# Keys and low halves of the second sorted edge list, made at the end of the first graph layer's loop instead of at the head of its dense part

## The reference

```python
# 1: first graph layer, 50000 edges sorted by destination
xn = layernorm(x)
new_x = segment_sum(edge_weight[:, None] * xn[src], dst, 3125)
out1 = new_x @ hamilton1
out1 = tanh(batchnorm(out1) * gamma + beta)
x = x + out1 @ hamilton2
# 2: gated experts, the gate by attention over a second list of 32768 edges
src2, dst2 = L0_ffn_edge_index
h = layernorm(x) @ W_gat
e = leaky_relu(a_src[src2] + a_dst[dst2]); alpha = softmax of e over each dst2
agg = segment_sum(h[src2] * alpha, dst2); scores = mean(layernorm(agg))
x = x + sum over the top 2 of 4 experts of w * (gelu(xn @ W1 + b1) @ W2 + b2)
# 3: attention over the first edges; 4: sparse experts, 2 of 16
```

## Time and profile before

| | us |
|---|---|
| median of 3 runs | 2825.48 |
| lowest, highest | 2815.58, 2832.08 |
| the profiled execution | 2822.73 |
| its span | 2820.9 |

### The profile page before, as it was taken

The page is one execution under the profiler, slowest core; times in us unless marked ns, Lnnn a source line. Parts: engine busy times, 40 slices in busy tenths (PEclk is TensorE's granted clock), DMA queues, the critical chain, the costliest instruction groups (busy, mean ns, idle before and its releaser), DMA issues. The chain is left out here.

```text
span 2820.9 us, 49472 instructions
## 1 busy us (share of the span) xinstructions
PE 2125.6 (75%) x10310; PEld 1616.9 (57%) x10311; DVE 1787.4 (63%) x4382; ACT 1123.3 (40%) x2764; POOL 1529.9 (54%) x1278
## 2 busy tenths in 40 slices
PE   4587777877776278999996767777777775679990
PEld 2465555655554156777784435555555554569990
DVE  5466677777668353333535848888888887654436
ACT  0354444444442042222323126666666662213332
POOL 0288888888887201777530037777777770025550
PEclk8677787787777587999997888999999998769995
DMA  7577777778777621232124457676666673532225
GB/s 250 150 111 127 120 128 132 124 126 128 130 119 103 155 66 51 46 75 61 45 77 159 149 169 207 194 203 200 201 196 201 199 197 97 190 125 70 71 67 187
DMA packets 257818, 381.37 MB, mean 135 GB/s; under 512 B 36246, under 2 KB 186181, under 8 KB 257477
## 3 DMA queue, kind: packets, MB, share of 16 engines
q0 software_dynamic: 109808, 194.70, 34.0%
q1 hardware_dynamic: 128021, 155.22, 18.3%
q10 hardware_dynamic: 19904, 30.41, 3.1%
HBM read 264.28 MB, written 115.94 MB: 135 GB/s over the span
## 5 line engine op out<-in xcount | busy, mean ns | idle before, releaser
L1006 POOL DMA_INDIRECT sum_tab<-Vs,spot x416 | 684.6, 1646 | 163.5 <-issue 100.1
L2424 POOL DMA_INDIRECT KV<-kv_tab,iS x448 | 472.6, 1055 | 183.6 <-issue 110.3
L893 PE MATMUL psV<-XN,Bs 128*128 x832 | 327.4, 506 | 167.9 <-issue 149.5
L893 PEld LDWEIGHTS psV<-XN,Bs 128*128 128x128 f32 x832 | 160.2, 233 | 306.1 <-issue 299.9
L2612 PE MATMUL psO<-msg,hot 128*128 128x264 f32 x896 | 228.5, 399 | 77.6 <-DVE agg L2532 56.3
L2600 PE MATMUL psQ<-Qs,hotT 128*128 x904 | 241.5, 414 | 56.2 <-issue 38.7
L972 ACT COPY Vs<-psV 128x512 f32<-128x512 f32 x208 | 121.6, 586 | 296.4 <-DMA sum_tab<-Vs,spot 242.8
L2612 PEld LDWEIGHTS psO<-msg,hot 128*128 128x128 f32 x896 | 165.4, 194 | 129.1 <-issue 104.8
L2600 PEld LDWEIGHTS psQ<-Qs,hotT 128*128 128x128 f32 x904 | 172.4, 203 | 108.8 <-issue 82.1
L1393 POOL DMA_INDIRECT ST<-h_tab,src x192 | 183.9, 958 | 58.5 <-issue 58.5
L2462 DVE TENSOR_TENSOR KV<-KV,psQ 128x1024 f32<-128x1024 f32 x112 | 136.7, 1221 | 77.4 <-issue 36.8
(11 more groups left out here) (592 smaller groups left out, 4380.6 us busy)
## 6 DMA issues: line engine op xcount, KB each, us to landing
kb<-key_rows SPq DMA_DIRECT2D x104, 256.0 KB
lowB<-low_tab SPq DMA_DIRECT2D x30, 512.0 KB
sum_tab<-zeros ACTq DMA_DIRECT2D x52, 256.0 KB, 3.0
parts<-sum_tab SPq DMA_DIRECT2D x20, 640.0 KB
ye_tab<-Ye SPq DMA_DIRECT2D x20, 640.0 KB, 3.5
Y<-ye_tab SPq DMA_DIRECT2D x20, 640.0 KB
lowB<-sort_tab SPq DMA_DIRECT2D x23, 384.0 KB, 6.0
keyB<-sort_tab SPq DMA_DIRECT2D x22, 384.0 KB, 5.3
```

Source lines behind the costliest of these rows:

```text
L893: ins = nc.tensor.matmul(psV[:, r % 2, x, :], Bs[:, q % 2, 2 * h + x, :], XN[:, bass.ds(t, 1), :].rearrange("p a d -> p (a d)"), start=Tru ...
L1006: pool.indirect_dma_start(out=sum_tabs[k], out_offset=bass.IndirectOffsetOnAxis(ap=spot[:, s, u:u + 1], axis=0), in_=Vs[:, j % VR, :], in_ ...
L2424: pool.indirect_dma_start(out=KV[:, s, u, :], out_offset=None, in_=kv_tab, in_offset=bass.IndirectOffsetOnAxis(ap=iS[:, s, u:u + 1], axis= ...
```

## The change

`sorted_keys` is gone, with its 26 VectorE instructions, its products, its iota and SP's store in the dense part. Its work stands at the end of `gnn0_phase`'s block: on VectorE between the copy of the gates and the wait for `sorted_` (the one-hots) and behind the writing of `src2` (the rest), on TensorE behind the closing product of the sort, on SP between the store of the gates and the wait for the two stores before it. Its tiles have no room of their own; they lie in `XN` (therefore the wait for `expanded`) and in `hot`. The two long 32-bit comparisons become 25 pairs of short ones with 16-bit input and output, with the iota that the sort already has (`iota_h`). The cast of the low halves comes before the flags; it came behind them. The sums are taken in `psL` and `psH`, which the sort has finished with.

```diff
@@ gnn0_phase, tiles
+                room, room_i, room_h = (XN[:, :, :].rearrange("p t d -> p (t d)").bitcast(d) if d != F32 else XN[:, :, :].rearrange("p t d -> p (t d)")
+                                        for d in (F32, I32, F16))
...
+                low_rows = room_h[:, at:at + T]
+                grid_row = room_h[:, at + T:at + T + NT * P].rearrange("p (t e) -> p t e", e=P)
+                grid_col = hot[:, :, :, :].rearrange("p s i e -> p (s i e)").bitcast(F16)[:, 0:NT * T].rearrange("p (t e) -> p t e", e=T)
...
@@ SP
                         sp.dma_start(gate_tab, gates[:, :, :, :].rearrange("g n h i -> g (n h i)")).then_inc(pens_out, 16)
+                        sp.wait_ge(lows_made, 1)
+                        sp.dma_start(sort_tabs[1][0:E2].rearrange("(b j e) -> j b e", j=P, e=P), low_rows.rearrange("p (b e) -> p b e", e=P)).then_inc(lows_out, 16)
                         sp.wait_ge(pens_out, 32)
+                        sp.wait_ge(lows_out, 16)
@@ VectorE
                         dve.sem_inc(gates_s, 1)
+                        dve.wait_ge(expanded, 2 * QB * TRIPS)
+                        c.inc(v.memset(oneT, 1.0))
+                        c.inc(v.tensor_scalar(lowp, iota_part[:, :], -1.0, None, ALU.add))
+                        c.seq(v.tensor_copy(firsti, first[:, :]))
+                        c.inc(v.tensor_scalar(shift, iota_free[:, :], lowp, None, ALU.is_equal))
+                        c.inc(v.tensor_single_scalar(parti[:, 0, :], firsti[:, 0:NT], 8, ALU.logical_shift_right))
+                        c.seq(v.tensor_single_scalar(parti[:, 1, :], firsti[:, 0:NT], T - 1, ALU.bitwise_and))
+                        c.seq(v.tensor_copy(grid_part, parti))
+                        for t in range(NT):
+                            c.inc(v.tensor_scalar(grid_row[:, t, :], iota_h[:, 0:P], grid_part[:, 0, t:t + 1], None, ALU.is_equal))
+                            c.inc(v.tensor_scalar(grid_col[:, t, :], iota_h[:, :], grid_part[:, 1, t:t + 1], None, ALU.is_equal))
+                        c.wait()
+                        dve.sem_inc(hots, 1)
                         dve.wait_ge(sorted_, 1)
                         c.seq(v.tensor_scalar(pay_out[:, :], psP[:, 0:T], float(HALF), None, ALU.add))
+                        c.seq(v.tensor_single_scalar(lowi, pay_out[:, :], P - 1, ALU.bitwise_and))
+                        c.seq(v.tensor_copy(lowf, lowi))
+                        dve.sem_inc(lows, 1)
+                        dve.wait_ge(gridded, 1)
+                        c.inc(v.tensor_reduce(total, psL[:, 0:T], AX, ALU.add))
+                        c.seq(v.tensor_copy(starts, psL[:, 0:T]))
+                        dve.sem_inc(totals, 1)
+                        dve.wait_ge(runs, 1)
+                        c.seq(v.scalar_tensor_tensor(before, psH[:, 0:1], -1.0, total, ALU.add, ALU.subtract))
+                        c.seq(v.tensor_tensor_scan(steps, oneT, starts, before, ALU.mult, ALU.add))
+                        dve.sem_inc(stepped, 1)
+                        c.inc(v.tensor_copy(key_out[:, :], steps))
+                        c.seq(v.tensor_scalar(tmp, iota_part[:, :], float(P - 1), -2.0, ALU.is_equal, ALU.mult))
+                        dve.wait_ge(lows_turned, 1)
+                        v.tensor_copy(low_rows, psL[:, 0:T]).then_inc(lows_made, 1)
+                        dve.wait_ge(shifted, 1)
+                        c.seq(v.tensor_tensor(nextf, psH[:, 1:2], tmp, ALU.add))
+                        run_flags(dve, c, steps, nextf, T, keep, pen, cont, tmp)
@@ TensorE
                         nc.tensor.matmul(psP[:, 0:T], zeroh[:, 0:P], zeroh[:, :], start=False, stop=True).then_inc(sorted_, 1)
+                        pe.wait_ge(hots, 1)
+                        for t in range(NT):
+                            ins = nc.tensor.matmul(psL[:, 0:T], grid_row[:, t, :], grid_col[:, t, :], start=(t == 0), stop=(t == NT - 1))
+                        ins.then_inc(gridded, 1)
+                        pe.wait_ge(totals, 1)
+                        nc.tensor.matmul(psH[:, 0:1], upper[:, :], total, start=True, stop=True).then_inc(runs, 1)
+                        pe.wait_ge(lows, 1)
+                        for n in range(2):
+                            ins = nc.tensor.transpose(psL[:, n * P:(n + 1) * P], lowf[:, n * P:(n + 1) * P], ident[:, :])
+                        ins.then_inc(lows_turned, 1)
+                        pe.wait_ge(stepped, 1)
+                        nc.tensor.matmul(psH[:, 1:2], shift, steps[:, 0:1], start=True, stop=True).then_inc(shifted, 1)
@@ the dense part
-        def sorted_keys(block, sb, ps, sem, first, key_out, keep, pen, cont, src, lows_made):
...
-                keys_on_vector, keys_on_tensor, low_rows = sorted_keys(block, sb, ps, sem, first, key_out, keep, pen, cont, src, lows_made)
...
-                        sp.wait_ge(lows_made, 1)
-                        sp.dma_start(sort_tabs[1][0:E2].rearrange("(b j e) -> j b e", j=P, e=P), low_rows[:, :].rearrange("p (b e) -> p b e", e=P)).then_inc(lows_out, 16)
-                        sp.wait_ge(lows_out, 16)
...
-                        keys_on_vector(dve)
...
-                        keys_on_tensor(pe)
```

More of the change, by code:

```diff
@@ L556, in gnn0_phase @@
         def gnn0_phase(srcI, dlI, wI, tile_row, key_rows, XN, tile_u, goal_rows, H, gam, bet,
-                       keyC, lo, hi, carried, first, endrow, none_row, firstrow, pay_out):
+                       keyC, lo, hi, carried, first, endrow, none_row, firstrow, pay_out, key_out, keep, pen, cont):
             ctx, sb, ps, sem = phase()
@@ L608, in gnn0_phase @@
                     sem(n) for n in ("ready", "chain", "built", "ranked", "weighed", "b_done", "b_out", "expanded", "rows_out", "placed"))
+                room, room_i, room_h = (XN[:, :, :].rearrange("p t d -> p (t d)").bitcast(d) if d != F32 else XN[:, :, :].rearrange("p t d -> p (t d)")
+                                        for d in (F32, I32, F16))
+                firsti, parti = room_i[:, 0:NH], room_i[:, NH:NH + 2 * NT].rearrange("p (a t) -> p a t", a=2)
+                at = NH + 2 * NT
+                grid_part = room[:, at:at + 2 * NT].rearrange("p (a t) -> p a t", a=2)
+                at += 2 * NT
+                starts, steps, oneT, lowf = (room[:, at + n * T:at + (n + 1) * T] for n in range(4))
+                lowi = room_i[:, at + 4 * T:at + 5 * T]
+                shift = room[:, at + 5 * T:at + 5 * T + P]
+                total, before, nextf, tmp, lowp = (room[:, at + 5 * T + P + n:at + 5 * T + P + n + 1] for n in range(5))
+                at = 2 * (at + 6 * T + P)
+                low_rows = room_h[:, at:at + T]
+                grid_row = room_h[:, at + T:at + T + NT * P].rearrange("p (t e) -> p t e", e=P)
+                assert at + T + NT * P <= 2 * NT * D and NT * T <= 4 * GI * P
+                grid_col = hot[:, :, :, :].rearrange("p s i e -> p (s i e)").bitcast(F16)[:, 0:NT * T].rearrange("p (t e) -> p t e", e=T)
+                hots, gridded, totals, runs, stepped, shifted, lows, lows_turned, lows_made, lows_out = (
+                    sem(n) for n in ("hots", "gridded", "totals", "runs", "stepped", "shifted", "lows", "lows_turned", "lows_made", "lows_out"))
                 minus = {(1, 0), (2, 0), (3, 0), (2, 1), (3, 2), (1, 3)}
@@ L1084, in gnn0_dense @@
-        def gnn0_dense(H, gam, bet, first, key_out, keep, pen, cont, src, XNT, w_dram, PN, sink):
+        def gnn0_dense(H, gam, bet, XNT, w_dram, PN, sink):
             ctx, sb, ps, sem = phase()
@@ L1110, in gnn0_dense @@
                 with nc.Block() as block:
-                    lows_made, lows_out = sem("lows_made"), sem("lows_out")
-                    keys_on_vector, keys_on_tensor, low_rows = sorted_keys(block, sb, ps, sem, first, key_out, keep, pen, cont, src, lows_made)
                     @block.sync
@@ L2969, in bass_gnn_moe_kernel @@
                         gnn0_phase(srcI, dlI, wI, tile_row, key_rows, XN, tile_u, goal_rows, H0, gam0, bet0,
-                                   keyC, loC, hiC, carriedC, firstC, end2, E2, first2, src2)
+                                   keyC, loC, hiC, carriedC, firstC, end2, E2, first2, src2, dst2, keep2, pen2, cont2)
                     r_ctx = h_ctx
@@ L2974, in bass_gnn_moe_kernel @@
                     HG = keep_sb(r_ctx, "HG", [P, NT, 24])
-                    gnn0_dense(H0, gam0, bet0, firstC, dst2, keep2, pen2, cont2, src2, XNT0, f0_wgat, 16, HG[:, :, 8:24])
+                    gnn0_dense(H0, gam0, bet0, XNT0, f0_wgat, 16, HG[:, :, 8:24])
                     gat_phase(HG, XNT0, b1T0, cont2, end2, G0)
```

## The result

| | before | changed |
|---|---|---|
| median of 13 runs, us | 2824.45 | 2814.34 |
| lowest, highest | 2815.58, 2832.08 | 2807.21, 2820.22 |
| the profiled execution, us | 2822.73 | 2820.22 |
| its span, us | 2820.9 | 2818.4 |

The ratio is 0.9961, 95% interval 0.995 to 0.9971: 10 us less. The forecast was 2816, with a change within 0.5%. The two profiled executions differ by 2.5 us only, since that of the changed kernel is at the upper end of its runs. So I read stretches in it, each against its own start, and not the span.

The account below looks back on a forecast made before the run. No engine is full; POOL's scatters bound the tail, and VectorE's head, then the loads, bound the dense part's start. 10.2 us gained less 0.6 lost gives 9.6, so 2825.5 becomes 2815.9 us, range 2807 to 2825.

Parts of the forecast that it names:

- The head's worth: Dense part's start: removing 20.75 us of VectorE work gains 10.2 us, the rest going into waits for groups 0 and 1.
- landing times taken from groups 2 and 3: Dense part's loads: groups 2 and 3 were taken 10.05 and 17.57 us after issue, so groups 0 and 1 would be too.
- the steps: Dense part's loads: each later group lands 7.52 to 8.73 us after the one before, taken as 8.0.
- The tail: End of the first graph layer's block: moved work ends at 939.3 on VectorE, hidden beside POOL's scatters and drain until 949.8.
- its store: SP's 64 KB store of low halves, moved to the tail: up to 7.3 us to land, there at 946.6.
- POOL: Tail's 13 scatter issues, the path there: 0.6 us lost to VectorE's moved work, between 0 and 4.3.
- the small operations: Tail's VectorE operations other than the pairs, 5.8 us busy: charged 0.6 us of POOL's time.
- The rival: Tail: the comparison burst holds POOL, up to 15.6 us lost, total 5.4 us slower at 2831; chance 5%.
- the 5.94 us issue: A POOL issue of 5.94 instead of 1.55 us, beside a two-tensor 32-bit comparison and a 32-bit scalar operation; evidence for POOL being held.
- The clock: Dense part: TensorE's granted clock moves; gain falls to 1 us (2824, 13%) or rises to 12.6 us (2813, 8%).
- the sum: Whole kernel: 10.2 us gained at the head less 0.6 lost on POOL, 9.6 us in all.
- the limit: Whole kernel: a measurement tells about 0.5%, 14.1 us, from no change; a result within it was given 78%.

Follow-up runs that it names:

- three profiles: The changed kernel, first measured and then repeated twice unedited, against the kernel before: ratios 0.9961, 0.9957 and 0.9959.
- The two heads put back: Changed kernel with 10.3 or 20.6 us of unused comparisons added at the dense part's head: 2814.51 and 2824.20 us, ratios 0.9971 and 1.0008 to the kernel before.
- third profile: The changed kernel's third run, unedited, against the kernel before: 2812.74 us, ratio 0.9959.
- the long comparisons of the experiment: Changed kernel with two long 32-bit comparisons in the tail instead of the 16-bit pairs: 2821.36 us, ratio 0.9988 to the kernel before.
- an edit about 750 us ahead of it: Changed kernel without the tail's work, with keys, flags and carry filled with constants: 2881.82 us, ratio 1.0204 to the kernel before.

## Why the prediction was right

- *The head's worth.* The forecast was 10.2 us by landing times taken from groups 2 and 3 of the kernel before, bounds 8.0 to 11.6. Counted from the first load, group 4 came 10.2, 9.8 and 9.8 us earlier in three profiles. The two heads put back show the reason directly: in the stretch 10 us cost nothing, 20 cost 10. Two errors nearly cancel here: the steps were 7.6, 7.5 and 8.1 us (8.4 and 8.5 for the last in the other two profiles), where I took 8.0 each; groups 0 and 1 were taken at 10.7 and 18.4, not 10.05 and 17.57.
- *The tail.* VectorE was forecast to end at 939.3 and ended at 938.8. That is luck, since three errors cancel: it began 2.4 us later than before (918.6 for 916.2), and the pairs took 9.7 us (0.39 each) where the twelve of the sort, which also multiply, had suggested 11.3, and the products 4.4 for 5.7. SP waited 1.3 us for its store behind the issuing (2.4 in a third profile), not up to 7.3.
- *POOL.* I charged 0.6 us, all for the small operations, and nothing for the pairs. In the first profile it was 0.3, on the pairs; in the third about 0.6, half of it on an issue beside the scan. The rival would have needed 10.2 us of loss. The prediction's reading of the 5.94 us issue was only half sound. The rule that the prediction took from the Trainium skill, "SBUF — State Buffer", section "Who interferes with whom", is that for copies, casts and scalar operations in a two-port mode. Of the two operations beside that issue the longer (3.92 us) compares two tensors, as do the long comparisons of the experiment; the statement on two inputs, cited there, is the one that fits them. The short pairs, which the two-port rule would concern, lengthened an issue by 0.09 us at most, and whether they run in such a mode no run shows.
- *The clock*, given 21% as two cases, is where the stretch behind group 4 lost part of its time: 95.3 us before; 97.8, 94.9 and 96.5 in three profiles of the changed kernel. In the first, TensorE's clock fell to 0.67 at the first of the last group's first products, where it was 1.00 before. Eight of them took 3.62 us for 2.32, and the last of them ended 1.5 us later behind group 4's addition. In the third it was the same (0.66, 3.56 us); in the second there was no fall and no loss. The kernel before has such a slow eight too (3.68 us, at 993.12), but two groups earlier, where VectorE still waits for loads.

```profile
1001.00:1006.00 5.00, 4.81 (x15) 3.34 (x15) 0.00 (x0) 1.45 (x4) 0.00 (x0) 0.67 0.00 0
```

Over the whole stretch it is a matter of -0.4 to 2.5 us, of either sign, and the mean over three is 1.1 us lost. What makes up the rest of the 2.5 stays open. So by the profiles the dense part gained 7.7, 10.2 and 8.6 us, 8.8 in the mean; the medians say 10.1. That the forecast's 9.6 is within half a microsecond of the medians is partly luck: the sum left the clock out, and 1.3 us of the medians' gain stand in no stretch that was read.
- *What the total could tell.* The interval of the ratio, 0.3 to 0.5%, lies within the 0.5% that the prediction named as the limit, as forecast.

## What to carry to other kernels

Work at a stage's head costs only what exceeds the wait that would stand there anyway. Find that wait in the same stage's later rounds (here 10.05 us from a pair of loads to its first use) before you count the head's length as the gain, and prove it by putting idle work back. When work is moved beside GpSimd's scatters, its form decides: two long comparisons of two 32-bit tensors held two scatters for 7.8 us, fifty short 16-bit ones for 0.3 in all. And an experiment that shortens a program can change how a loop far behind it is fetched; look at the instruction queue's packets before you believe its total.

## What the runs showed of the hardware that I had not expected

- An untouched loop ran some 67 us slower after an edit about 750 us ahead of it, with 60 packets of instructions fetched within it for 5, and a stall of 5.1 to 5.8 us about every 54 us.
- For a 64 KB store to DRAM SP waited 1.3 us once it was issued (at 937.2, in 0.4 us) on a quiet queue; behind the loads it had waited 7.3 us for it.
- The same kernel's loop ends up to 12 us apart in its profiled executions (first load at 947.4, 953.2 and 959.0), while from there to group 4 it repeats within 0.4 us.
